# Hyperbolic attention: transposed weights copied one unit later and first in DVE's step, value products and divisions one step later

## The reference

```python
q, k, v = (qkv[0], qkv[1], qkv[2])
tq, sq = _expmap0_split(q)
tk, sk = _expmap0_split(k)
neg_inner = jnp.einsum('bhie,bhje->bhij', tq, tk) - jnp.einsum('bhid,bhjd->bhij', sq, sk)
dist = jnp.arccosh(jnp.maximum(neg_inner, 1.0 + 1e-07))
scores = -dist ** 2 / np.sqrt(D)
scores = jnp.where(causal[None, None], scores, -jnp.inf)
attn = jax.nn.softmax(scores, axis=-1) * spike_mask
y = jnp.einsum('bhij,bhjd->bhid', attn, v)
```

## Time and profile before

| | |
|---|---|
| median of three executions | 4466.02 us (4456.5 to 4469.49) |
| the profiled execution | 4458.36 us |
| its span, first to last instruction | 4456.6 us |
| PE busy | 3514.0 us (79%) |
| DVE busy | 2255.7 us (51%) |
| ACT busy | 1635.7 us (37%) |
| POOL busy | 919.0 us (21%) |
| stage "Da", from its first score matmul | at 476.6, 1445.8, 2415.2 and 3381.2 us |

### The profile page before, as it was taken

The page is one execution under the profiler, slowest core; times in us unless marked ns, Lnnn a source line. Parts: engine busy times, 40 slices in busy tenths (PEclk is TensorE's granted clock), DMA queues, the critical chain, the costliest instruction groups (busy, mean ns, idle before and its releaser), DMA issues. The chain is left out here.

```text
span 4456.6 us, 58459 instructions
## 1 busy us (share of the span) xinstructions
PE 3514.0 (79%) x22310; PEld 1971.3 (44%) x22310; DVE 2255.7 (51%) x4289; ACT 1635.7 (37%) x2451; POOL 919.0 (21%) x993
## 2 busy tenths in 40 slices
PE   3887778898887688888886688988876788955995
PEld 2423453436324355245334445255234534345884
DVE  2465766552465855634556765624657665530111
ACT  0343643242443733332344732423445532411221
POOL 0101542001202722011104611011115421021002
PEclk9988789998998799999897799999887899977998
DMA  4111102100203011101112012011111021024453
GB/s 77 36 54 71 15 2 78 47 20 20 76 14 85 1 40 43 44 28 48 43 30 67 1 41 67 19 38 37 54 71 15 1 75 51 20 98 155 165 173 125
DMA packets 242705, 238.79 MB, mean 54 GB/s; under 512 B 111870, under 2 KB 207852, under 8 KB 239980
## 3 DMA queue, kind: packets, MB, share of 16 engines
q1 hardware_dynamic: 234224, 217.91, 16.4%
q0 software_dynamic: 3072, 8.39, 0.6%
q10 hardware_dynamic: 5116, 8.58, 0.6%
HBM read 166.15 MB, written 68.68 MB: 53 GB/s over the span
## 5 line engine op out<-in xcount | busy, mean ns | idle before, releaser
L842 ACT ACTIVATE prob<-psum 128x1024 f32<-128x1024 f32 x384 | 372.2, 1021 | 548.4 <-PE psum L762 548.4
L1173 ACT ACTIVATE prob<-psum 128x1024 f32<-128x1024 f32 (+3 forms) x384 | 331.2, 914 | 435.0 <-PE psum L1093 435.0
L883 DVE TENSOR_REDUCE scr<-psum 128x1 f32<-128x512 f32 x576 | 371.4, 685 | 204.8 <-PE psum L749 200.6
L1211 DVE TENSOR_REDUCE stats<-psum 128x1 f32<-128x512 f32 (+3 forms) x576 | 334.0, 620 | 162.1 <-PE psum L1081 157.4
L380 PE MATMUL psum<-ident 128*128 128x128 f32 x2464 | 303.6, 284 | 16.6 <-PEq L69 8.9
L380 PEld LDWEIGHTS psum<-ident 128*128 128x128 f32 x2464 | 297.2, 200 | 28.1 <-issue 27.2
L1093 PE MATMUL psum<-stack 32*128 32x512 f32 (+3 forms) x1536 | 210.2, 618 | 64.8 <-ACT prob L1173 34.8
L759 PE MATMUL psum<-stack 32*128 32x512 f32 x1536 | 226.4, 659 | 31.1 <-DVE xo L873 24.7
L790 PE MATMUL psum<-prob,ones_f 128*32 128x512 f32 x1536 | 204.8, 601 | 0.0
L1108 PE MATMUL psum<-prob,vbig 128*32 128x512 f32 (+3 forms) x1536 | 188.9, 565 | 4.3 <-ACT prob L1173 4.3
L2469 PE MATMUL psum<-xgT,ew 128*128 128x256 f32 x736 | 167.7, 387 | 18.0 <-DVE xgT L2515 18.0
(11 more groups left out here) (429 smaller groups left out, 6729.2 us busy)
## 6 DMA issues: line engine op xcount, KB each, us to landing
ew<-in_L_ffn_W SPq DMA_DIRECT2D x46, 1024.0 KB, 7.5
stack<-q_terms SPq DMA_DIRECT2D x144, 128.0 KB, 2.4
w_mlp<-in_L_xattn_a_li_w SPq DMA_DIRECT2D x16, 1024.0 KB, 6.3
q_terms<-parts SPq DMA_DIRECT2D x96, 128.0 KB, 2.1
stack<-k_terms SPq DMA_DIRECT2D x72, 128.0 KB, 2.7
w_mlp<-k_terms SPq DMA_DIRECT2D x36, 256.0 KB, 4.5
w_mlp<-a_terms SPq DMA_DIRECT2D x36, 256.0 KB, 4.7
a_keys<-stack SPq DMA_DIRECT2D x4, 2048.0 KB, 7.2
```

The source lines that it names most:

```text
L842: act.activation(prob[:, i % 4, :, :], psum[:, 2 * p:2 * p + 2, :], ACT.Exp, scale=scale).then_inc(exped, 1)
L883: dve.tensor_reduce(found[:, c:c + 1], ring(i), AX.X, ALU.max).then_inc(freed, 1)
L1173: act.activation(prob[:, i % 4, :, q0:T], psum[:, 2 * p:2 * p + 2, q0:T], ACT.Exp, scale=scale).then_inc(exped, 1)
L1211: dve.tensor_reduce(found[:, c:c + 1], ring(i)[:, 0:keys_of(t)], AX.X, ALU.max).then_inc(freed, 1)
```

## The change

Five distances change, and one place within a body. On PE `weigh` goes from i-4 to i-5, `gather` and the spreading of inverses one step further too. On DVE `copy_first` goes from i-3 to i-4 and to the head of the body; `lift`, `invert` and `divide` go one step further. On ACT `copy_second` goes from i-3 to i-4 and stays last. The loops get one more step. No instruction is added or removed, no buffer is changed.

```diff
--- before.py
+++ after.py
@@ -2006,17 +2006,17 @@
             score(0)
             if last_unit[0] == 0:
                 score(1)
-            for i in range(NU + 7):
+            for i in range(NU + 8):
                 if i + 1 < NU and i + 1 in last_unit and units[i + 1][0] + 1 < len(quads):
                     score(units[i + 1][0] + 1)
                 if 0 <= i - 3 < NU:
                     turn(i - 3)
-                if 0 <= i - 4 < NU:
-                    weigh(i - 4)
-                if i - 5 in ends:
-                    gather(ends.index(i - 5))
+                if 0 <= i - 5 < NU:
+                    weigh(i - 5)
                 if i - 6 in ends:
-                    e.spread_inverses(pe, ends.index(i - 6), inverted, spread_in)
+                    gather(ends.index(i - 6))
+                if i - 7 in ends:
+                    e.spread_inverses(pe, ends.index(i - 7), inverted, spread_in)
 
         @block.vector
         def _(dve):
@@ -2061,20 +2061,20 @@
 
             above_one(0)
             times_itself(0)
-            for i in range(NU + 8):
+            for i in range(NU + 9):
+                if 0 <= i - 4 < NU:
+                    copy_first(i - 4)
                 if i + 1 < NU:
                     above_one(i + 1)
                     times_itself(i + 1)
                 if 0 <= i - 2 < NU:
                     square(i - 2)
-                if 0 <= i - 3 < NU:
-                    copy_first(i - 3)
-                if i - 5 in ends:
-                    lift(ends.index(i - 5))
                 if i - 6 in ends:
-                    e.invert(dve, ends.index(i - 6), gathered, inverted)
+                    lift(ends.index(i - 6))
                 if i - 7 in ends:
-                    e.divide(dve, then, ends.index(i - 7), spread_in, divided)
+                    e.invert(dve, ends.index(i - 7), gathered, inverted)
+                if i - 8 in ends:
+                    e.divide(dve, then, ends.index(i - 8), spread_in, divided)
 
         @block.scalar
         def _(act):
@@ -2117,7 +2117,7 @@
                     act.wait_ge(weighed, i - 1)
                 act.copy(turned_w[i % 2][:, T:n], psum[:, 5, 0:n - T]).then_inc(copied_b, 1)
 
-            for i in range(NU + 3):
+            for i in range(NU + 4):
                 if i < NU:
                     log_of_square(i)
                 if 0 <= i - 1 < NU:
@@ -2126,8 +2126,8 @@
                     root(i)
                 if 0 <= i - 2 < NU:
                     exponentiate(i - 2)
-                if 0 <= i - 3 < NU:
-                    copy_second(i - 3)
+                if 0 <= i - 4 < NU:
+                    copy_second(i - 4)
 
         @block.gpsimd
         def _(pool):
```

## The result

The changed kernel takes 4788.7 us (median; 4784.8 to 4800.6), the kernel before 4467.6 us, a ratio of 1.073 [1.070, 1.076]. It is 321 us slower. The forecast was 4705 us with a range of 4590 to 4790: the sign and the mechanism held, and the time was 84 us too low. The median itself lies 1 us inside the range, but 1.073 times the 4466 us that the forecast starts from is 4792 us, just beyond its upper end: the loss was larger than the range allowed.

What follows compares the result with a forecast made beforehand. Latency between engines was taken as the bound. Ring, ends, savings and clock summed to 205.6 us a stage against 145.9; four times +59.7 (+239) on 4458.4, plus 7.6, gave 4705 us, range 4590 to 4790.

Steps and rivals of the forecast that it cites:

- What bounds the kernel, and that DVE's copy does not move: Stage Da: no engine is full, latency between engines counts; DVE's first copy keeps its place among squares and maxima.
- The ring: Stage Da: ACT's later second copy closes a chain of waits through PE and DVE; 190.8 us for 24 units.
- The signs that it named: Stage Da: PE waits 60 us or more, ACT some 80, DVE over 80; steps 7 to 10 us; clock below 0.70.
- Its price on DVE is 0: Head-group ends ahead of DVE's next copy cost nothing; without cover at most 2.8 us for each of 16 groups.
- The squares, 48.7 us: DVE's squares in stage Da keep their stalls behind POOL's products: 48.7 us, not the undisturbed 28.
- The low bound: All stalls of DVE's squares gone and PE at full clock: 170 us a stage, 4561 us in all.
- PE's clock ... I add 5 us: PE idles some 4 us of each 8 in the ring, so its clock drops: 5 us a stage added.
- the upper bound: No narrow-unit savings, transposes at the low clock, products at their slowest: 227 us a stage, 4791 us in all.
- Seams and narrow units, -13 us: Stage Da: overlaps between neighbours on an engine save 4 us, units 0, 6 and 12 with four blocks save 9.
- Milder ring: Rival: the same ring, but DVE's squares meet POOL less often; 4561 to 4625 us, chance 0.10.
- no change: Rival: the ring has unseen slack, ACT having long waits of its own; 4453 to 4479 us, chance 0.03.
- faster: Rival: DVE's 25.0 us a stage of waiting for transposes go; 4366 us at best, chance 0.03.

Runs made afterwards that it cites:

- e1: Changed kernel with ACT's second copy alone put back one step earlier; 4483.1 us, ratio 1.005.
- e2: Kernel before with ACT's second copy alone moved one step later; 4676.7 us, ratio 1.047.
- e8: Changed kernel with three buffers for transposed weights instead of two; 4652.0 us, ratio 1.041.
- e5: Changed kernel with POOL's 16 z*z products made by ACT, ahead of its exponentials; 4728.2 us, ratio 1.058.
- e7: Changed kernel with ACT's second copy ahead of the exponentials in the same late step; 4536.9 us, ratio 1.016.
- e11: Changed kernel with ACT's second copy put back one step and three buffers for transposed weights; 4446.2 us, ratio 0.995.
- e9: Changed kernel with 12 or 7 idle matrix products on PE in a step while it waits; 4733.0 us, ratio 1.060.
- e4: Changed kernel with 20 idle matrix products on PE in each step while it waits; 4815.7 us, ratio 1.080.

## Why the prediction was right in kind and wrong in size

*What bounds the kernel, and that DVE's copy does not move.* Right. No engine's busy time decides, and the order on DVE is that of before for copies, maxima and squares. A reader of the diff alone would have looked for the effect there.

*The ring.* Right. That ACT's second copy closes it is shown by e1 and e2; that the value products are a link, by e8; the squares, by e5; the point where it opens, by e7. ACT's scale and exponentials, the copies and the maxima are links by the timeline and by the sum, not by a run of their own. The signs that it named came: PE waits 58.7 us for L2118 (60 or more was said), ACT 99.9 (80), DVE 97.6 with L1997 by name, the clock 0.58, and 331 of 342 us inside the four stages. One came in part: most steps last 7 to 10 us, but in the first stage two last 12.1 and one 10.9, and the last two 5.5 and 2.3.

*"Its price on DVE is 0".* Borne out by the rows, though no run has it alone. Even behind the slowest of these four instructions in the ring, 2.28 us, DVE waits another 2.18 us for the value products before its copy at 640.55, and e11, with these instructions where the change puts them, is not slower than the kernel before. The "at most 2.8 us" for a group without cover rests on no row: undisturbed the four take 2.0 us, and 3.9 with the 2.28.

*The squares, 48.7 us.* Right: 50.1 us. The low bound would have been wrong, and e5 shows what it takes to get there.

*"PE's clock ... I add 5 us".* This is the step that failed. The term measures 14.8 us in the first stage (68.5 us for transposes and products instead of the 53.7 that the sum started from) and 18 us in the others. The prediction had all it needed: it said that PE would idle 4 us of each 8, it had eight transposes at 1.97 us behind an idle time of 2.39, and it priced the low level at +7.5 and +10 us, but put it in the upper bound, took for the transposes a value between the two levels and added nothing for the products. In the ring nearly every step of PE comes behind such an idle time, so the upper bound, 227 us a stage, was the estimate; its clock term of 17.5 us in all is what the four stages have in the mean, 17.3. That 226.6 us lands right beside it is in part luck: it saves 4 us for seams and narrow units where 5.7 were saved, and lacks the squares' 1.3 us. The Trainium skill, "TensorE: Matmul & The Clock Gate", part on the HAM clock gate, has the rule that speaks for this, and the forecast had quoted it; but it applied the rule to the transposes alone and left the value products out. The trace agrees with the rule for both, and e9 shows that they are links: 16.7 us a stage come back with the clock.

*Seams and narrow units, -13 us.* The second term that was mis-sized. In the first stage 19.4 + 206.6 + 5.3 - 1.9 = 229.4 us stand against 223.7 measured, so they save 5.7 us. The seams save little or nothing: PE takes over 0.14 us after ACT's copy (637.75 to 637.89), and DVE 0.12 to 0.14 us after the value products (640.42 to 640.55), not 0.05. The forecast's 0.05 came from rows in which DVE copies behind transposes, where it is 0.04 us in all 16 waits of the first stage before. The steps behind units 6 and 12 were 6.6 and 8.1 us long instead of about 9.4, so these two save 4 us and not 6; the remaining 1.7 us are for unit 0 and the seams together.

Together, for the first stage: 205.6 forecast, +9.8 clock, +7.3 seams and narrow units, +1.0 squares and the rest, 223.7 measured. The other stages have 3 to 4 us more clock. They also started from 142.7 to 143.5 us and not from 145.9, which a sum over the first stage alone did not see: 8 us in all. So the four stages grew by 331 us and not by 239: 84 us by the terms of the sum (4 x 21.0), 8 by the start.

*The rivals.* "Milder ring", "no change" and "faster" are out. The last two rested on slack in ACT; ACT's 99.9 us of waiting shows that it has plenty, but PE's transposes wait for one instruction in its queue, not for its time.

## What to carry to other kernels

In a pipeline whose engines each follow a fixed order, ask of a moved instruction not how long it takes but what now stands ahead of it in its queue, and who waits for it. If that leads back to work which waits for the same consumer, the pieces form a ring that goes round once a unit, and its length is the sum of the busy times of all its links and of the handovers between them, however idle each engine is. Take these links at the clock and with the stalls that the new rhythm gives them. Here PE waited some 4 us for the second copy (58.7 us in 14 waits), the granted clock was 0.58, and all of PE's work in the ring was near its price at the low level.

## What the runs showed of the hardware that I had not expected

- A 128x128 fp32 matrix product that is no transpose takes 0.236 us at full clock (20 in 4.73 us, e4), a transpose 0.13 us (eight in 1.04 us there).
- PE's transposes start 0.14 to 0.15 us after ACT's second copy in the changed kernel, where PE idles at a granted clock of 0.58. In e9 and e4, where idle products keep PE running, it is 0.05 us whenever these products are done in time.
- DVE's copy that spreads the inverses (L1253, 128x512 with a repeated input, one input in SBUF) took 0.43 us in 14 of its 16 runs in the kernel before. In the changed kernel eight of 16 stand just behind the squares, beside POOL's addition, and take 1.20 or 2.28 us:

```profile
578.43 1.20 DVE L1253 COPY scr<-inverse 128x512 f32<-128x512 f32 x1
577.64 1.71 POOL L2148 TENSOR_TENSOR parts<-parts,prob 128x512 f32<-128x512 f32 x1
636.09 2.28 DVE L1253 COPY scr<-inverse 128x512 f32<-128x512 f32 x1
635.29 2.79 POOL L2148 TENSOR_TENSOR parts<-parts,prob 128x1024 f32<-128x1024 f32 x1
```

Each ended 0.3 us after POOL's instruction. Two in the kernel before did the same, at 0.71 us, and in e5, where no instruction of POOL runs beside them, all 16 took 0.43 us. The Trainium skill, "SBUF — State Buffer", section "Who interferes with whom", has a one-input copy in a two-port mode and GpSimd exclude each other as well; these rows agree, though no view shows in which mode the copy ran.
